# Bias products padded from 3 and 8 rows to 128, and a rewritten table of turns, in a four-layer decoder kernel

## The reference

```python
# L0 attention: v has a bias, and so has the output
x = x + (softmax_like(q, k) @ (xn @ Wv + bv)) @ Wo + bo
# L1 attention: the output has a bias
x = x + heads(xn) @ Wo + bo
# L2 attention and L2 cross-attention: bias of v, bias of the output
x = x + attend(q, k, xn @ Wv.T + bv) @ Wo.T + bo
# L3 cross-attention: bias of v;  L3 feed-forward: bias of the router's logits
V = ctx @ Wv + bv
logits = xn @ W_router + b_router            # 8 experts
# L2 and L3 feed-forward: each expert has an output bias, weighted by the router
out = out + cw[:, e:e + 1] * (h @ w2[e].T + b2[e])
```

## Time and profile before

| | |
|---|---|
| median of 3 runs | 2390.73 us (2388.62 to 2390.85) |
| profiled execution | 2394.86 us, span 2392.7 us |
| mean granted clock of TensorE over the span | 0.932 |
| PE busy | 2070.8 us, 87% of the span, 15996 records |
| DVE, ACT, POOL busy | 1443.9, 1107.6, 229.0 us |
| `banks<-rows,ones` on PE | 144 records |
| `banks<-b2rows,wT` on PE | 64 records |

### The profile page before, as it was taken

The page is one execution under the profiler, slowest core; times in us unless marked ns, Lnnn a source line. Parts: engine busy times, 40 slices in busy tenths (PEclk is TensorE's granted clock), DMA queues, the critical chain, the costliest instruction groups (busy, mean ns, idle before and its releaser), DMA issues.

```text
span 2392.7 us, 41882 instructions
## 1 busy us (share of the span) xinstructions
PE 2070.8 (87%) x15996; PEld 1623.9 (68%) x15996; DVE 1443.9 (60%) x4778; ACT 1107.6 (46%) x2842; POOL 229.0 (10%) x190
## 2 busy tenths in 40 slices
PE   7687999999994776779997889999999977779999
PEld 5455785666662553548885666666899855658998
DVE  5587426777774765867767567665333465566554
ACT  2276426665663664662223544555544455422222
POOL 3300000000002000001102000000111252110000
PEclk9799999999996888999997989999999988979999
DMA  4224100000007677761004222330000023220000
GB/s 156 74 68 112 54 1 1 1 1 2 1 1 214 189 210 207 204 186 71 1 1 101 63 73 71 87 81 2 1 1 1 21 68 95 63 89 10 5 5 8
DMA packets 169312, 155.57 MB, mean 65 GB/s; under 512 B 10628, under 2 KB 157852, under 8 KB 168472
## 3 DMA queue, kind: packets, MB, share of 16 engines
q1 hardware_dynamic: 169112, 152.89, 23.1%
HBM read 89.06 MB, written 63.39 MB: 64 GB/s over the span
## 4 chain that ended last, share of the span: by engine, by line
PE 62%; DVE 15%; DMA 10%; ACT 7%; SPq 3%; issue 2%; POOL 1%; ACTq 0%; DVEq 0%
PE banks L602 57%; DMA stacks<-region 5%; ACT P L1292 3%; SPq L2299 3%; DMA skew<-region 3%; PE banks L915 2%; DVE region L1667 2%; DVE P L1604 2%; ACT region L1292 1%; DVE P L1837 1%; DVE region L1604 1%; DVE region L1907 1%; DVE negm L1615 1%; DVE P L1857 1%; PE banks L766 1%
## 5 line engine op out<-in xcount | busy, mean ns | idle before, releaser
L602 PE MATMUL banks<-xnT,region 128*128 128x256 f32 x1696 | 436.5, 391 | 7.6 <-ACT xnT L1292 4.1
L602 PEld LDWEIGHTS banks<-xnT,region 128*128 128x128 f32 x1696 | 313.7, 195 | 53.5 <-ACT xnT L1292 7.1
L1292 ACT ACTIVATE P<-P,negm 128x256 f32<-128x256 f32 x512 | 253.8, 498 | 107.5 <-DVE negm L1857 68.9
L1292 ACT ACTIVATE kz<-banks,perm 128x256 f32<-128x256 f32 x400 | 167.8, 470 | 258.6 <-PE banks L602 256.5
L602 PEld LDWEIGHTS banks<-region,kz 128*128 128x128 f32 x2304 | 276.7, 193 | 11.0 <-DVE x L1612 2.4
L602 PE MATMUL banks<-region,kz 128*128 128x128 f32 x2304 | 280.3, 276 | 3.2 <-DVE x L1612 2.5
L1292 ACT ACTIVATE P<-banks 128x512 f32<-128x512 f32 (+2 forms) x392 | 183.5, 512 | 138.9 <-PE banks L602 136.9
L2183 POOL TENSOR_TENSOR rstd<-rstd,pows 128x2 f32<-128x2 f32 x96 | 68.2, 710 | 1765.1 <-DVE rstd L1608 1765.0
L1612 DVE SCALAR_TENSOR_TENSOR x<-banks,w,x 128x128 f32<-128x128 f32 x256 | 77.9, 346 | 189.7 <-PE banks L602 178.2
L1615 DVE TENSOR_REDUCE negm<-banks 128x2 f32<-128x512 f32 (+1 forms) x264 | 146.2, 589 | 49.3 <-PE banks L602 47.7
L602 PE MATMUL banks<-kz,qs 128*128 128x256 bf16 (+1 forms) x512 | 127.5, 284 | 25.7 <-DVE negm L1615 10.4
(11 more groups left out here) (240 smaller groups left out, 4019.7 us busy)
## 6 DMA issues: line engine op xcount, KB each, us to landing
stacks<-region SPq DMA_DIRECT2D x178, 192.0 KB, 3.1
skew<-region SPq DMA_DIRECT2D x64, 256.0 KB, 3.3
qs<-stacks SPq DMA_DIRECT2D x24, 408.0 KB
kz<-stacks SPq DMA_DIRECT2D x48, 192.0 KB
skew<-region SPq DMA_DIRECT2D x64, 128.0 KB, 2.8
skew_room<-skew SPq DMA_DIRECT2D x32, 256.0 KB, 3.5
P<-skew SPq DMA_DIRECT2D x32, 256.0 KB, 3.6
region<-stacks SPq DMA_DIRECT2D x34, 192.0 KB, 3.0
```

What stands on the lines that cost most here:

```text
L602: return p.e.matmul(o, lhsT, rhs, start=start, stop=stop)
L1292: return a.e.activation(o, i, f, **kw)
```

## The change

1. `rows3` and `b2rows` get 128 partitions, of which the DMAs fill 3 and 8 as before; the others are zero. `ones3` (3 partitions) becomes `ones_b` (128 partitions of ones). `wT` had 128 partitions already; ACT still writes only its first 8, and the product now reads all.
2. POOL zeroes `rows3` (128x1032 bfloat16), `b2rows` (128x256 float32) and both `wT` (128x256 float32) at the start; SP waits for these fills before it copies the three rows of the bias.
3. `TURNS` is another table for each of the five engines.

```diff
-    b2rows = sbuf("b2rows", [E, width("b2")])
+    b2rows = sbuf("b2rows", [128, width("b2")])
-    rows3 = sbuf("rows3", [3, row_parts * ROW], BF16)
+    rows3 = sbuf("rows3", [128, row_parts * ROW], BF16)
-    ones3 = sbuf("ones3", [3, 128], BF16)
+    ones_b = sbuf("ones_b", [128, 128], BF16)
...
-                        i = mm(o, ones3[:, :], bias, False, True)
+                        i = mm(o, ones_b[:, :], bias, False, True)
...
-                    i = mm(s.S0[:, t * D:(t + 1) * D], s.wT[0:E, t * 128:(t + 1) * 128], b2)
+                    i = mm(s.S0[:, t * D:(t + 1) * D], s.wT[:, t * 128:(t + 1) * 128], b2)
...
         g.e.memset(pows[:, :], -0.5).then_inc(consts_sem, 1)
-        g.e.memset(ones3[:, :], 1.0).then_inc(consts_sem, 1)
+        g.e.memset(rows3[:, :], 0.0)
+        g.e.memset(b2rows[:, :], 0.0)
+        for s in streams:
+            g.e.memset(s.wT[:, :], 0.0)
+        g.e.memset(ones_b[:, :], 1.0).then_inc(consts_sem, 1)
...
         d.wait_ge(tables, ROW_CUT)
+        d.wait_ge(consts_sem, ZERO_ROWS)
         for k in range(3):
             dma(rows3[k:k + 1, :], row_cut[:, k, :], bias_sem)
...
-        load("b2", b2rows[:, :], dram["pack_b2"])
+        load("b2", b2rows[0:E, :], dram["pack_b2"])
...
 TURNS = {
-    "tensor": ("11114200220012007100310017002200120041005100170012002200110031005700220022001100410025110022001100220010400104"
+    "tensor": ("11114200220012006100310027002200120071004300260011001200710023002600110012005010012001100504002100114010300102"
```

More of the change, by code:

```diff
@@ new lines @@
+    "gpsimd": ("3l1100110011j0110011002200110011001100110011004100140011001100110011001100110011001100220010101201201002012010"
+        "02011090010933001100110011001100110011001100101001011010101001011050010111053200110011002200120011101010111010"
+        "010150100101010100100503001"),
+    "sync": ("29110011j02100110034002200110033006600660b21001220200200300120010010031002002001200102220200530032002500550055"
+        "005300ac220011202002003010201003212200200502005200330022005500530032002300ah3120013001202020202022020010040300"
+        "4200520032002500550033002200a51003100c1200202021500140033200230032002200320025005500330022009n0050610011001210"
+        "04013010100104002010300105105001030013102100110021010200301001003101040050100501009871001300210011001200448004"
+        "ga008o001200110011001"),
@@ L556, in program @@
     REL_FULL, PLACE_FULL = 1, 2
-    POWS, ONES3 = 1, 2
+    POWS, ZERO_ROWS = 1, 2
     VW_ONES = [3, 4]
@@ L802, in L0_attn @@
                 mm(s.T[:, t * D:(t + 1) * D], s.xnT[:, t * 128:(t + 1) * 128], W1["L0a_v"], True, False)
-                i = mm(s.T[:, t * D:(t + 1) * D], ones3[:, :], RW["L0a_vb"], False, True)
+                i = mm(s.T[:, t * D:(t + 1) * D], ones_b[:, :], RW["L0a_vb"], False, True)
             i.then_inc(s.T_full, 1)
@@ L1245, in L3_xattn @@
                 mm(s.T[:, t * D:(t + 1) * D], s.ctxT[:, t * 128:(t + 1) * 128], P["L3x_v"], True, False)
-                i = mm(s.T[:, t * D:(t + 1) * D], ones3[:, :], RW["L3x_vb"], False, True)
+                i = mm(s.T[:, t * D:(t + 1) * D], ones_b[:, :], RW["L3x_vb"], False, True)
             i.then_inc(s.T_full, 1)
```

102 lines of the change are left out of this document (72 added, 30 removed).

## The result

| | median us | against the kernel before |
|---|---|---|
| before | 2390.79 (2388.62 to 2394.52, 4 runs) | |
| changed | 2351.52 (2348.47 to 2357.04, 4 runs) | 0.9837 [0.9815, 0.9859] |

The account below looks back on a forecast made before the run. PE was taken to bound most stages: 43 us less on it, 30.3 reaching the end. With -3, -6 and -2 for the order and +1 for the start, -40.3 in all, forecast 2350 us, range 2328 to 2380.

Parts of the forecast that it names:

- the chain's shares: PE's share of the chain in each stage, 0.48 (L3x) to 0.94 (L3f), taken as the part of PE's saving reaching the end.
- The price of a bias product: Wide 3-row products between float32 records: padding to 128 rows saves 0.24 us each at full clock, bounds 0.10 and 0.29.
- What of it reaches the end: L0a to L3f: of 43 us less on PE, 30.3 reach the end, weighted by stage.
- The order: New TURNS table: -3 for 24 fewer changes of shape, -6 for L0x with L0f, -2 in the last 29 us.
- its largest term: L0x: mixing stream 1's last item with stream 0's L0f fills PE's idle time, -6 us, bounds 0 and -15.
- the rival with the order worth more: The order takes back 13 us idle in L0x and 15 to 20 in L1x: 2325 us, chance 0.12.
- The term for the end: L3f: both streams alternate to the end, taking back 2 of 4.4 us that PE idles in the last 29.
- The wait for the positions: L1a's first item reads the table of relative positions; two L0f items cover its DMA: nothing, up to 13 us uncovered.
- The start: POOL's added zero fills and larger ones_b take 1.6 us and move the start by +1 us, bounds 0 and 1.6.
- The waits take it up: PE only waits longer for ACT, DVE and the stacks, so less of the saving counts: 2373 us, chance 0.18.
- Weight loads in the open: Padded bias products occupy all rows, so weight loads of 0.1 us stand between products: 20 us back, 2370, chance 0.04.
- Slower by L1x: Streams in unison add PE waits for ACT in L1x, 34 more: 2409 us, chance 0.04; decided from 23 further waits.

Follow-up runs that it names:

- the hybrid: The changed kernel with the new TURNS table only up to the start of L1x on every engine, the old table from there: 2344.73 us, ratio 0.9816.

## Why the prediction was right

The time came out 1.5 us from the forecast. The cost of a change of shape and the chain's shares were rightly read. The rest of the closeness is luck: the order's total had the right size for a wrong reason, and errors in both directions cancel.

- *The price of a bias product*: 0.24 forecast, 0.58 - 0.33 = 0.25 measured; the router 0.20 forecast, 0.18 measured. At half clock 0.40 was forecast and 0.30 measured, and for a run of the expert bias 0.37 against 0.19 on its own four records (what the record behind it gains is not in that). With the measured prices the prediction's sum gives 39 us on PE in place of 43, and 27 at the end in place of 30.3. Yet PE's busy time fell by 50.2 us with padding alone. The clock is part of that: L0a ran at 0.99 in that execution and at 0.92 before. An estimate from the mean clocks of the two spans, 2070.8 x (1 - 0.932/0.939), puts it at 15 us. The Trainium skill ("TensorEngine Tiling (Array Packing)", section "Key Properties", with the 128 cycles of "TensorE: Matmul & The Clock Gate", section "Step-by-step: what each phase is for") gave an estimate of 53 ns a change and 17 us on PE. The trace does not agree: at full clock a product with two changes costs 0.25 us more than one with none, 0.12 a change. The rows had it right: about 0.1 us a change, and the record behind it delayed as well.
- *What of it reaches the end*: 30.3 less 1 of the start, 29.3 forecast, 27.7 measured. 9.2 of it in L0 and L1 (8.3 by the terms and the start as measured), 18 in L2 and L3 (20.8). The shares of the chain by stage were good weights for the sum. For single stages one pair of profiles is too coarse to say.
- *The order*: -3, -6 and -2 were forecast, -11; 14.3 and 11 were measured. But it is made up otherwise, and **the mechanism of its largest term was wrong**. The prediction said that L0f's products, mixed with the last item of L0x, would take back 6 us of idle time. The mixing gave at most 1: 12.3 of the 13.3 us were gone before L0f's first product, in the waits for L0x's mask and `picks`. Their size lies within the bounds of the term (0 to -15) and is what the rival with the order worth more had for L0x, 13. For the changes of shape (forecast 3) the busy time of PE shows 3.6 in one pair of profiles and 4 over six, not parted from the clock. **The term for the end failed**: I forecast 2 us from the idle time of the last 29 us, and PE is busy there for 24.4 us after and 24.7 before:

```profile
2318.00:2347.00 29.00, 24.37 (x179) 22.68 (x177) 10.95 (x30) 4.61 (x12) 0.00 (x0) 1.00 0.03 10
```

  And "for the rest the order is a local reshuffle, and I price it at nothing" hid a loss of 5 to 8 us after L1a (5 by the ratios of the change and the hybrid, 8.4 side by side). The gain before L1x that was forecast too small, the end and this loss cancel.
- *The wait for the positions*: no wait of PE for `rel_vec` appears; the DMA took 10.2 us and L0f covered it.
- *The start*: +1 forecast, 13.69 - 12.51 = 1.2 measured. I took POOL's fills as a chain of their own and did not see that they hold DVE up.

The rivals. *The waits take it up* (2373): it would have left padding alone near 2378, and that took 2362 (0.9884, where 2378 would be 0.9947, outside the interval). *Weight loads in the open*: the 0.05 us from a padded product to the next leaves no room for a load of 0.1 that is not hidden. The rule of the Trainium skill ("TensorE: Matmul & The Clock Gate", section "The mechanism") that a load overlaps only where its row group differs does not agree with these rows, in which all tiles have 128. The same section also lets a load go ahead that targets the background weight buffer; no row shows which buffer a load used. *Slower by L1x*: PE's waits in L1x (702:1071), beside the earlier trace rows:

```profile
PE banks L604 <- ACT region L1294: 52.0, 38, 5.9
```

Eight waits more but no more time, and L1x took 369 us for 361, within the 10 forecast. The point of 23 further waits was not reached.

## What to carry to other kernels

- A short product that accumulates between others should have their tile shape, even if most of its rows are zeros. Find its price from start to start, over the record behind it as well; durations show nothing (0.22 us either way). Padding to 64 rows between products of 128 left the period as it was.
- Weigh what an engine saves by its share of the chain in each stage, not of the whole span. For an order, find each wait that it removes and where it stood, and look for what it loses later: cut the table at the stages and run the halves. An effect of 4 us needs several profiles or many runs.
- Constant fills at the start belong on an engine that has nothing to do then. Look at what runs beside them: here POOL's fills held up DVE's first casts.

## What the runs showed of the hardware

- A product whose tile has another shape than its neighbours' costs 0.25 us at full clock (period 0.58 against 0.33), and 0.30 at half speed (0.94 against 0.64). With 64 rows in place of 3 it is the same 0.58.

- A cast or a `TENSOR_SCALAR` of DVE that runs beside a fill of POOL ends within 0.1 us of the fill's end: 0.17 to 0.22 us became up to 1.85. A `TENSOR_TENSOR` beside a fill keeps its 0.17. A fill goes by its number of elements: `qs` (128x2048 bfloat16) takes 1.80 us on POOL, and `v` with 1024 float32 elements in the same bytes 0.97. On DVE `qs` takes 0.91, where it is written as 1024 32-bit elements:

```profile
2.38 0.91 DVE L2175 MEMSET qs<- 128x1024 uint32 x1 [0.16 <-issue]
```

- The granted clock of a stage of the same code differed between executions: 0.97 and 0.99 in L1a, 4 us. A difference of a few us in one stage of two profiles is not yet a finding.
